# VectorE's order in the tile loop of an attention and expert kernel: four low parts ahead of the output additions, and two normalisation blocks more on VectorE

## The reference

```python
x = x + autocorrelation(layernorm(x), ctx, ctx)
y = layernorm(x)
scores = (y @ Wq.T) @ keys.T                         # 16 numbers, then 64, per token
top_vals, top_idx = top_k(scores, 16)
gate = sum(one_hot(top_idx, 64) * softmax(top_vals)[..., None], axis=-2)
z = (y @ A.T).reshape(..., 64, 8) * gate[..., None]  # 512 numbers per token
x = x + (z.reshape(..., 512) @ B.T) * 2              # ALPHA / TOP_K = 2
```

## Time and profile before

| | before |
| --- | --- |
| median of three runs | 2111.95 us (2111.89 to 2114.59) |
| the profiled execution | time 2114.59 us, span 2112.8 us |
| TensorE busy | 2073.7 us, 98% of the span |
| VectorE busy | 1962.4 us, 93% |
| ScalarE busy | 1442.6 us, 68% |
| GpSimd busy | 1566.3 us, 74% |
| granted TensorE clock, mean of the core | 0.998 |

### The profile page before, as it was taken

How to read it: one execution, slowest core, us unless ns; L and a number is a source line. 1 busy time by engine, 2 the same in 40 slices (tenths; PEclk the granted TensorE clock), 3 DMA queues, 4 the chain that set the end, 5 groups by cost and what they waited for, 6 DMA issues and landing times.

```text
span 2112.8 us, 28855 instructions
## 1 busy us (share of the span) xinstructions
PE 2073.7 (98%) x8472; PEld 1281.2 (61%) x8472; DVE 1962.4 (93%) x4331; ACT 1442.6 (68%) x3191; POOL 1566.3 (74%) x965
## 2 busy tenths in 40 slices
PE   5999999999999999999999999999999999999999
PEld 2455455445445545545544544688888888888887
DVE  7999999999999999999999999978899999999983
ACT  4687787687687687787766545766666666666761
POOL 6899999999999999999999997843344434443330
PEclk9999999999999999999999999999999999999999
DMA  7233232233333323323213216645555545555531
GB/s 283 75 138 105 85 135 101 104 125 110 105 108 126 105 97 138 105 85 138 96 65 105 90 45 237 227 170 176 182 178 172 179 171 179 186 170 177 180 130 60
DMA packets 110704, 287.49 MB, mean 136 GB/s; under 512 B 7168, under 2 KB 7296, under 8 KB 109568
## 3 DMA queue, kind: packets, MB, share of 16 engines
q1 hardware_dynamic: 110592, 286.19, 39.0%
HBM read 219.06 MB, written 67.11 MB: 135 GB/s over the span
## 4 chain that ended last, share of the span: by engine, by line
PE 56%; DVE 20%; POOL 16%; issue 5%; ACT 2%; DMA 1%; DVEq 0%; SPq 0%; POOLq 0%; ACTq 0%
PE out L595 6%; PE out L596 6%; PE out L597 6%; POOL r_f L1865 5%; PE z L595 5%; PE z L597 5%; PE z L596 5%; PE pair L763 4%; PE pair L769 3%; DVE prod L1068 3%; DVE prod L1072 3%; POOL half_fold L1854 2%; PE pair L658 2%; PE evac L669 2%; PE evac L670 2%
## 5 line engine op out<-in xcount | busy, mean ns | idle before, releaser
L769 PE MATMUL pair<-r_f,back 128*128 128x512 f32 x768 | 342.8, 597 | 0.5 <-DVE prod L1072 0.5
L1899 POOL TENSOR_TENSOR rows<-rows,cin 128x1024 f32<-128x1024 f32 x48 | 118.6, 2470 | 286.5 <-DMA rows<-out_dram 226.9
L1865 POOL TENSOR_TENSOR r_f<-prod 128x1024 f32<-128x1024 f32 x128 | 303.0, 2378 | 11.8 <-DVE prod L1070 9.2
L769 PEld LDWEIGHTS pair<-r_f,back 128*128 128x128 f32 x768 | 143.0, 190 | 192.8 <-issue 146.5
L1565 ACT ACTIVATE xn<-rows,shift,rstd 32x512 f32<-32x512 f32 x280 | 227.8, 814 | 7.5
L763 PE MATMUL pair<-w_sb,wts 128*128 128x512 f32 x512 | 227.6, 598 | 1.2 <-ACT w_sb L1682 0.8
L1031 DVE TENSOR_SCALAR xn<-rows,rstd,shift 32x512 f32<-32x512 f32 x168 | 197.2, 1174 | 5.6
L595 PE MATMUL out<-b_hi,zt_hi 128*128 128x512 f32 x492 | 197.5, 401 | 0.0
L595 PE MATMUL z<-a_hi,xt 128*128 128x512 f32 x496 | 196.2, 396 | 0.0
L597 PE MATMUL z<-a_hi,xt 128*128 128x512 f32 x496 | 193.4, 390 | 0.0
L596 PE MATMUL z<-a_lo,xt 128*128 128x512 f32 x496 | 193.1, 389 | 0.0
(11 more groups left out here) (238 smaller groups left out, 5559.9 us busy)
## 6 DMA issues: line engine op xcount, KB each, us to landing
out_dram<-att_sb SPq DMA_DIRECT2D x32, 1024.0 KB, 4.2
rows<-out_dram SPq DMA_DIRECT2D x64, 512.0 KB, 3.9
cin<-out_dram SPq DMA_DIRECT2D x63, 512.0 KB, 4.4
xin<-in_x_dram SPq DMA_DIRECT2D x63, 512.0 KB, 4.2
vf<-in_ctx_dram SPq DMA_DIRECT2D x31, 1024.0 KB, 5.1
out_dram<-rows SPq DMA_DIRECT2D x62, 512.0 KB, 2.7
xf<-in_x_dram SPq DMA_DIRECT2D x30, 1024.0 KB, 5.4
stat_in<-in_x_dram SPq DMA_DIRECT2D x27, 1024.0 KB, 5.2
```

Source lines behind the costliest of these rows:

```text
L769: return nc.tensor.matmul(pair_ps[:, bank, :], back[:, 3 * bank + n, :], r_f[:, row, :], start=n == 0, stop=n == 2)
L1865: nc.gpsimd.tensor_tensor(dst, prod[:, slot, 0:2, :], prod[:, slot, 2:4, :], ALU.add).then_inc(add_done, 1)
```

## The change

The diff has four edits. The 16 normalisation blocks are split 8 and 8 by the partition group c, where ScalarE had 10 and VectorE 6. In the general step VectorE's four `tile_low` come before the second half of the statistics and before `add_out(1)`: the second ahead of `add_out(0)`, the third and fourth right behind it. `gate_z` keeps its place behind `add_out(1)` in the other steps; in the last tile's step (u = TT - 1 = 31), where it stood ahead of `add_out(0)`, it now stands behind `add_out(1)` too. The two waits at the head of ScalarE's `norm_blocks` are made conditional on its first block being of the group 0, which it always is.

```diff
-        BLOCKS = [(c, b) for c in range(4) for b in range(4)]
-        ACT_BLOCKS, DVE_BLOCKS = BLOCKS[:10], BLOCKS[10:]
+        ACT_BLOCKS, DVE_BLOCKS = (0, 1), (2, 3)
...
@@ VectorE, norm_blocks (ScalarE's is changed in the same way)
-                for c, b in blocks:
+                for c in blocks:
                     own = slice(SPREAD * c, SPREAD * (c + 1))
-                    nc.vector.tensor_scalar(by_block[SPREAD * b:SPREAD * (b + 1), :, c, :],
-                                            rows[slot][own, b * 512:(b + 1) * 512].rearrange("p (k i) -> p k i", k=KD),
-                                            rstd2[own], shift2[own], ALU.mult, ALU.add).then_inc(xn_part, 1)
+                    for b in range(4):
+                        nc.vector.tensor_scalar(by_block[SPREAD * b:SPREAD * (b + 1), :, c, :],
+                                                rows[slot][own, b * 512:(b + 1) * 512].rearrange("p (k i) -> p k i", k=KD),
+                                                rstd2[own], shift2[own], ALU.mult, ALU.add).then_inc(xn_part, 1)
...
@@ VectorE, tile_step, general step
                 if f:
                     tile_low(u + 1, 0)
-                if is_step(u, TT - 1):
-                    gate_z()
+                    tile_low(u + 1, 1)
                 add_out(0)
                 if f:
-                    tile_low(u + 1, 1)
+                    tile_low(u + 1, 2)
+                    tile_low(u + 1, 3)
                 if later_tile(u):
                     half_statistics(u + 2, (r + 3) % RING, 1)
                     tile_mean(u + 2)
                 add_out(1)
                 if later_tile(u):
                     invert_root(u + 2)
-                if f:
-                    tile_low(u + 1, 2)
-                    tile_low(u + 1, 3)
-                if f:
+                if a:
                     gate_z()
                 if is_step(u, TT - 1):
                     zt_low(TT)
                 add_out(2)
                 add_out(3)
                 if ahead(u):
                     norm_blocks(u + 2, (r + 3) % RING, DVE_BLOCKS)
...
@@ ScalarE, norm_blocks
-                act.wait_ge(norm2_ready, 2 * t + 2)
-                act.wait_ge(tp_lo, tp_at(t - 1, 3) + 1)
+                if blocks[0] == 0:
+                    act.wait_ge(norm2_ready, 2 * t + 2)
+                    act.wait_ge(tp_lo, tp_at(t - 1, 3) + 1)
```

More of the change, by code:

```diff
@@ L1558, in norm_blocks @@
             def norm_blocks(t, slot, blocks):
-                act.wait_ge(norm2_ready, 2 * t + 2)
-                act.wait_ge(tp_lo, tp_at(t - 1, 3) + 1)
+                if blocks[0] == 0:
+                    act.wait_ge(norm2_ready, 2 * t + 2)
+                    act.wait_ge(tp_lo, tp_at(t - 1, 3) + 1)
                 by_block = xn[:].rearrange("p (k c i) -> p k c i", k=KD, c=4)
-                for c, b in blocks:
+                for c in blocks:
                     own = slice(SPREAD * c, SPREAD * (c + 1))
-                    nc.scalar.activation(by_block[SPREAD * b:SPREAD * (b + 1), :, c, :],
-                                         rows[slot][own, b * 512:(b + 1) * 512].rearrange("p (k i) -> p k i", k=KD),
-                                         ACT.Identity, bias=shift2[own], scale=rstd2[own]).then_inc(xn_part, 1)
+                    for b in range(4):
+                        nc.scalar.activation(by_block[SPREAD * b:SPREAD * (b + 1), :, c, :],
+                                             rows[slot][own, b * 512:(b + 1) * 512].rearrange("p (k i) -> p k i", k=KD),
+                                             ACT.Identity, bias=shift2[own], scale=rstd2[own]).then_inc(xn_part, 1)
             act.wait_ge(consts_set, 2)
```

## The result

The changed kernel takes 2144.88 us (median of three runs, 2141.78 to 2147.7), against 2111.95: a ratio of 1.0151, 95% interval 1.0126 to 1.0177. The forecast was 2144.6, slower.

A forecast was written before the change was run, and what follows sets the result against it. TensorE was taken to bound the kernel, then a loop through VectorE, store, load and GpSimd: 30.4 + 2.3 = 32.7 us over the median 2111.95 gives 2144.6. Range 2136 to 2158 for the full loop, 2119 to 2158 overall.

The forecast's parts named there:

- The two blocks cost nothing by themselves: VectorE's two added blocks cost 0.57 each, 1.15 us per tile, covered by its wait of 1.28.
- VectorE's wait ahead of its fourth add_out: Sign in the profile after: this wait, 1.28 us per tile before, stays as long or gets longer.
- The loop: Second add_out, store, load, GpSimd's additions, held tile_low, second add_out: 23.72 becomes 24.91, 1.17 over TensorE's period; chance 0.60.
- VectorE by its own sum: Rival: added blocks cost the mean 1.174 each, 1.07 too much per tile, 2144.2 us; TensorE waits ahead of the queries; 0.08.
- Only the tail: Rival: loop stays under TensorE's period, only the last gate's 2.3 us remains, 2114.3 us; chance 0.10.
- half the loop: Rival: first tile_low falls before GpSimd's fourth addition, only the second is held; 0.82 per tile, 2127 to 2136; chance 0.20.
- just fits: Claim that the loop's pieces before the change sum to 23.72 us against TensorE's 23.74.
- The size: Tiles u = 4 to 29: the loop costs 1.17 us in each of 26 tiles, 30.4 us.
- The wait stands ahead of the fourth bank: TensorE waits 1.17 us per tile for the second add_out at the fourth output bank, not ahead of the queries.
- What is held: GpSimd's additions hold two of eight blocks and the first tile_low, about 1.9 us; first addition 3.6 to 4.0 after the turning.
- The last gate: Step u = 31: gate_z behind the second add_out idles TensorE 2.3 us before the last turning; bounds 1.5 and 2.8.

The follow-up runs named there:

- blocks_only: The kernel before with the normalisation blocks split eight each on ScalarE and VectorE, nothing else of the change: 2113.09 us, ratio 1.0002.
- order_only: The changed kernel with the blocks split as before (ScalarE 10, VectorE 6), keeping the new tile_low order and late last gate: 2141.55 us, ratio 1.0135.
- one_low: The kernel before with only the third tile_low moved ahead of the second half of the statistics and the second add_out: 2113.4 us, ratio 1.0005.
- store_late: The kernel before with SP's store of the first output half waiting for the fourth tile_low instead of the second add_out: 2133.04 us, ratio 1.0091.
- tail_only: The kernel before with only the last tile's gate_z (u = 31) moved behind the second add_out: 2115.78 us, ratio 1.0014.
- short_fourth: The changed kernel with GpSimd's input addition for the second half of the rows cut to 64 of 1024 columns from the fifth tile on: 2115.95 us, 1.0013.
- early_add: The changed kernel with the second add_out moved ahead of the second half of the statistics and the mean, behind the four tile_low: 2119.5 us, 1.0034.
- early_add_10_6: early_add with the blocks split 10 and 6 as before, the last gate still where the change put it: 2114.42 us, ratio 1.001.
- one_low_8_8: The kernel before with the third tile_low moved as in one_low and the blocks split 8 and 8: 2127.14 us, ratio 1.0071.

## Why the prediction was right, step by step

**The two blocks cost nothing by themselves.** Right (blocks_only). Their price of 0.57 was right where two are held: six blocks last 7.36 and eight 8.49 in most tiles. The 0.45 by the page of after is a mean with tiles in it that have fewer held, and leaves out the 0.03 between two blocks. ScalarE's relief was worth nothing. What took them up was misread: the wait gave half and a shorter hold the rest (blocks_only), where the forecast had the wait alone. VectorE's wait ahead of its fourth add_out was to stay as long or get longer in after; it is 1.03 where it was 1.28, so that mark was wrong.

**The loop sets the pace.** Right, and shown from four sides: the store alone delayed (slower), the add_out advanced (recovered), the fourth addition cut (recovered), the blocks taken off (2141.55, nearly the same). VectorE by its own sum gave the same 2144 and would have passed unseen by the time alone; order_only decides against it. "Only the tail" and "half the loop" are out by the tiles' 1.265.

One step of the forecast proves less than it says. The 23.72 runs from one second add_out to the next, and at a steady pace that distance is the period of 23.74, however much slack lies between. Over the 26 tiles of before it is 23.74 in the mean, from 23.05 to 24.35. Where the loop is early, the second add_out waits for TensorE's bank, as in the tile at 1671.29 of before:

```profile
1689.79 0.69 DVE L1359 SCALAR_TENSOR_TENSOR rows<-out,rows 128x512 f32<-128x512 f32 x1 [0.83 <-PE out L597]
```

So "just fits" and a margin of 0.02 are not shown by that sum. That the loop is nearly full is shown by the pieces that follow each other without such a wait in most tiles, and by the runs: over the 26 tiles 1.19 more in it cost 1.27 per tile, 1.26 more at the store 0.71, but 0.6 more (one_low) only 0.02.

**The size.** The terms of the loop, means over the tiles from 1456 us to 2081 us:

| piece | forecast | measured |
| --- | --- | --- |
| second add_out to first addition | 6.71 | 7.03 |
| first addition to end of the fourth | 12.85 | 12.65 |
| from there to the second add_out | 5.35 | 5.32 |
| sum | 24.91 | 25.00 |

The first piece was mis-sized by 0.3, the second by 0.2 the other way. Why store and load take 0.3 more was not tried, and stays open. Over 26 tiles it is 32.9 where I had 30.4. In the profiled execution the sum is 32.9 + 2.3 + 1.7 = 36.9, against 32.7, and its time is 2148.67, against 2147.3 forecast; that the difference is only 1.4 is because the execution of before had lost 2.8 at its start. The median of the three runs lies 3.8 under this profiled execution. No trace shows where another execution is faster. That 2144.88 meets 2144.6 so closely is luck: the terms are not that good.

**The wait stands ahead of the fourth bank.** In part wrong. Counting what the first two products of a bank start later than 0.23 apart, the tile shown loses 0.86 at the fourth bank and 0.68 at the third; over 24 tiles the means are 0.82 and 0.38, of 1.26 a tile. The rows show why: on VectorE the two add_outs end 3.61 apart (1676.91 and 1680.52), and TensorE's bank of 12 products takes 2.75. So the fourth bank can't wait longer than 0.86 once the third has waited; what the loop has over that comes out at the first add_out, which is late because it stands behind the held tile_low. The forecast had these pieces of VectorE in its loop (3.01 between the two add_outs in before, 0.60 more for the tile_low that comes between them), but didn't compare their sum with the bank between.

**What is held.** Two of eight blocks, and the first tile_low with 2.13 in the mean (1.87 in the tile of the earlier trace rows, 1.9 forecast). The first addition comes 4.10 after the turning, 4.0 forecast. By the page SBUF — State Buffer of the Trainium skill (Who interferes with whom) the order of issue decides which of the two engines blocks. The trace agrees: the tile_low that meets a running addition ends 0.55 after it (one_low: 1588.21 after 1587.66), and the fourth addition, started at 1587.74 while that tile_low still ran, takes 2.72 instead of 2.39. The forecast also says that the trace shows add_out not held; in the tile it read, no add_out meets an addition. store_late shows it: an add_out that starts at 1692.61, inside GpSimd's addition from 1691.42 to 1694.24, takes 0.69, as it does alone.

**Half the loop.** The mechanism of this rival is what order_only and one_low do: once the blocks run free, the first tile_low meets the third addition. In order_only it brings 24.69, against 24.99 with eight blocks. The forecast gave the rival 2127 to 2136 by its terms and 2119 to 2136 in the chances; nothing stands behind the 2119 to 2127. I had set it aside as a matter of timing, where it was a matter of the other edit: the blocks decide which addition the first tile_low meets.

**The last gate.** 2.29 for 2.3. What the forecast left out is the stretch at half clock that can come after it, 1.7 us where it does.

## What to carry to other kernels

When two engines share something, ask of each move what it does to the whole cycle of buffer, store, load and addition, and compare that cycle with the period of the engine that bounds: here the cycle was nearly full while VectorE was busy for 92% of the tile and GpSimd for 41%. The distance between two occurrences of one event isn't that comparison; look in each piece for a wait on something outside the cycle. Two edits that are each free can be slow together, because one keeps the other from the order in which its cost is hidden, so they have to be priced in the state that both make. Where two theories give the same time, write down the wait that tells them apart before the result is known.

## What the runs showed of the hardware

An idle time of TensorE of 2.13 us was followed by a granted clock of 0.50 (1.2 GHz) for 3.41 us, starting 1.4 us after work had begun again (after: 2125.75 to 2129.16), where the same place in before has none. Its 1.7 us come on top of the 2.3 of the wait. tail_only has such a stretch from 2091.79, 0.1 us after work began again, order_only from 2120.17 and short_fourth from 2092.72. But the profiled executions of early_add and early_add_10_6 have the same idle time of 2.13 us and no such stretch behind it (a clock of 1.00, and 20.9 us from the last turning to the end of the span instead of 22.5). What decides isn't shown. In one_low_8_8 a wait of 1.94 us inside a tile was followed by one. The waits of up to 1.3 us in the tiles of after never were: their clock stays at 1.00. The page TensorE: Matmul & The Clock Gate of the Trainium skill (Part 1: The HAM clock gate) has the clock follow how busy the engine has been recently, which fits the stretches that follow a wait; no run here shows why two of the six executions with the same idle time have none.

The chain that ended last gives VectorE 42% of the span and TensorE 28% in after. That reads as if VectorE were the bound. A VectorE instruction that is held by GpSimd counts as busy, and the chain doesn't step over to GpSimd: between 1658 and 1684 it has no piece of GpSimd, and gives the hold of the first tile_low to VectorE and, for 2 us, to "issue". In order_only the same loop has VectorE idle for some 4 us per tile.
